# Wide attention of a two-layer decoder: the early maximum item placed behind the pass that subtracts the maxima

## The chip, the core and the metric

The kernel is one program on one NeuronCore of a Trainium2 chip. The metric is the time of one execution on the device in microseconds (us), and the figure for a kernel is the median over its runs. TensorE is called PE here, VectorE DVE, ScalarE ACT, GpSimd POOL, and PEld is TensorE's loading of weights.

## What is computed

The reference is a decoder of two layers over 1024 tokens of width 128, with a context of 6404 rows of width 96. Each layer is a self attention, a cross attention and a mixture of experts, each behind a layer norm and added to x. The change lies in the cross attention of the second layer, with 16 heads of width 64 ("wide"):

```python
q = query @ w_q                       # 1024 x 1024: 16 heads of 64
kv = context @ w_kv                   # 6404 x 2048
k, v = jnp.split(kv, 2, axis=-1)
scores = jnp.einsum('bhqd,bhkd->bhqk', q, k) * SCALE
attn = jax.nn.softmax(scores, axis=-1)
out = jnp.einsum('bhqk,bhkd->bhqd', attn, v)
return out @ w_out + b_out
```

## The kernel before

The stages run one after the other: self attention, first cross attention (small heads of 8), first experts, the second layer's attention over heads, and last `wide_heads_and_experts`, which holds the wide attention and the last experts. The wide attention takes about half of the time.

It works in 16 units. A unit is one pair of heads with one half of the tokens (512 queries), and has 51 steps, one for each block of 128 context rows, so there are 816 steps, taken in 408 pairs (`for j in range(0, STEPS, 2)`). Both heads of a pair lie in the 128 partitions, 64 for each head, and TensorE takes the two heads side by side. Query and key are each held as a high and a low part. The matmuls of one pair of steps, in program order before the change:

- `score(j)` and `score(j + 1)` (L2345): three products (high by high, low by high, high by low), each for two heads: 12 matmuls, with 64 rows of the array for each head, into PSUM banks 0 and 1 for one step and 2 and 3 for the other;
- the early item, `early[j // 2]`, when there is one: a maximum item (L2300), two matmuls of the same tiling as the scores, high part only, for a tile of 128 queries of the next unit against 512 keys. It goes to two of the three "side" banks (5 to 7), which are used in a ring;
- `subtract_maxima(j)` (L2358): four matmuls of 32 rows of the array each. They add minus the maximum to the four score banks, and their last ones release ACT by `scored`;
- `weigh(j - 2)` and `weigh(j - 1)` (L2371): probabilities times values, 128 rows by 64 columns of the array for each head, into bank 4; 8 matmul records for two steps;
- the whole items and the late items: `whole` holds now and then a fill of keys (`k`, L2318) or queries (`q`, L2311) for the next units, a turn of the maxima (`t`), a sum (`s`) or an output (`y`); `late[j // 2]` is the rest of this pair's maximum items, mostly one, in 20 places two or more.

A planner at the head of the function deals the 52 maximum items of each unit but the first out over the pairs of the unit before: 780 items, `early` takes the first of a pair (380 of them), `late` the rest (400). It also gives every item its place in the ring of three banks, in the order early, whole, late, pair after pair. A maximum item waits in `wait_place` until DVE has freed the banks, which means until the first of the two DVE reductions (L2555) of the maximum item before it, or the reading of the fill before it, is done. DVE takes, for each pair: the reductions of the early item, then an addition to the running sum (L2609) if the step is one of DVE's, the copy of the output at a unit's end (L2590), a piece of a reciprocal (L2584), then the work for the whole items (`k_lo`, L2569; `q_lo`, L2564; each behind ACT's copy of the high part, L2463 or L2460) and the reductions of the late items. ACT takes two exponentials (L2484) for each pair, then its copies for whole items. POOL adds most of the probabilities up (L2220). `score(j)` waits for the exponential of step j - 2, which used the same banks.

At the pair that follows the first step of a unit with an odd number (`between`), the late item stands between `weigh(j - 2)` and `weigh(j - 1)`, since the second has to wait until DVE has copied the last unit's output out of bank 4.

Of the kernel before, what the change touches and what calls it, by code (L numbers as in the profile page):

```python
# [1946 lines left out]
def wide_heads_and_experts(nc, name, net_name, PS, ident, ctxT, xn, xnT, x, O, A, values, out, wide):  # L1947
# [151 lines left out]
    def strip(s):  # L2099
        return slice(s * DH2, (s + 1) * DH2)  # L2100
# [4 lines left out]
    with ExitStack() as stack:  # L2105
# [160 lines left out]
        def _(pe):  # L2266
# [66 lines left out]
            def score(j):  # L2333
                n, kt = j // KT, j % KT
                p, hf, b = n // HALVES, n % HALVES, 2 * (j % 2)
                if j >= 2:
                    pe.wait_ge(exped, j - 1)
                if kt == 0:
                    pe.wait_ge(dve_freed, dve_count[("q", n)])
                if kt % 4 == 0 and hf == 0:  # L2340
                    pe.wait_ge(dve_freed, dve_count[("k", p, kt // 4)])
                keys = slice(kt * P, (kt + 1) * P)
                for k, q, start in ((k_hi, q_hi, True), (k_hi, q_lo, False), (k_lo, q_hi, False)):
                    for s in range(2):
                        pe.matmul(PS[:, b + s, :], k[p % 2][strip(s), keys], q[n % QBUFS][strip(s), :],  # L2345
                                  start=start, stop=False, tile_position=(s * DH2, 0))

            def subtract_maxima(j):

                for b in range(2):  # L2350
                    n, kt = (j + b) // KT, (j + b) % KT
                    if kt == 0:
                        pe.wait_ge(negated, negated_count[("t", n)])
                for b in range(2):
                    n, kt = (j + b) // KT, (j + b) % KT
                    for s in range(2):
                        r = 32 * (2 * b + s)
                        i = pe.matmul(PS[:, 2 * b + s, :], key_ones[r:r + 32, kt // (KT - 1), :],  # L2358
                                      minus_max[r:r + 32, n % 2, :], start=False, stop=True, tile_position=(r, 0))
                    i.then_inc(scored, 1)  # L2360

            def weigh(j):
                n, kt = j // KT, j % KT
                pe.wait_ge(exped, j + 1)
                if kt == 0 and n >= 1:
                    pe.wait_ge(out_copied, n)
                if kt % 4 == 0:
                    i = n * VF + kt // 4
                    pe.wait_ge(vals_loaded[i % VBUFS], 16 * (i // VBUFS + 1))
                for s in range(2):  # L2370
                    i = pe.matmul(PS[strip(s), PV, :], vals[:, value_slot(n, kt // 4), kt % 4, strip(s)],  # L2371
                                  prob[:, j % RING, s, :], start=(kt == 0), stop=(kt == KT - 1),
                                  tile_position=(0, s * DH2))
                i.then_inc(pv_done, 1)
# [7 lines left out]
            for j in range(0, STEPS, 2):  # L2382
                score(j)
                score(j + 1)
                for item in early[j // 2]:
                    side(item)
                subtract_maxima(j)
                between = j >= 2 and (j - 1) % KT == 0
                if j >= 2:
                    weigh(j - 2)  # L2390

                    if between:
                        assert not whole[j // 2]
                        for item in late[j // 2]:
                            side(item)
                    weigh(j - 1)
                for item in whole[j // 2] + ([] if between else late[j // 2]):
                    side(item)
                if j // KT == LAST:
                    if j % KT == NET["turn"]:  # L2400

                        pe.wait_ge(dve_freed, dve_count[("y", LAST - 1)])
                        pe.wait_ge(negated, negated_count[("s", LAST - 1)])
                        net.turn_tokens(pe, net.glue(0), 0)
                    if j % KT == NET["score"]:
                        net.score(pe, 0)
                    if j % KT == NET["turn_gates"]:
                        net.turn_gates(pe, 0)
                    if j % KT == NET["spread"]:
                        net.spread_gates(pe, 0, 0)  # L2410
# [536 lines left out]
```

## Time and profile before

| | us |
|---|---|
| median of 3 runs | 3848.77 |
| the runs | 3844.69, 3848.77, 3866.15 |
| span of the profiled execution | 3852.1 |
| mean granted TensorE clock over that span | 0.977 of full |

For the profiled execution only its span is given, from its first instruction to its last; what lies around that is not shown, and the span itself lies between the runs. In the page's slices the wide attention begins at about 1613 us with the maxima of its first unit; its steps, with maximum items beside them, go from 1667 to 3550 us, and the last unit, without maximum items, follows. A row of the timeline gives the start in us, how long the merged instructions took in us, engine, line, operation, what it writes and reads, the tile and how many; in square brackets stands idle time of the engine before it and what ended it. Matmuls are pipelined, so the durations overlap, and the distance between two starts is what a matmul takes of the engine.

### The profile page before, as it was taken

The numbers are of one execution on the slowest core, as the hardware profiler recorded it, in microseconds if no ns is written. First come the engines' busy times: TensorE is split into PE (matmuls) and PEld (weight loads), VectorE is DVE, ScalarE is ACT, GpSimd is POOL, SyncE is SP. The second block draws the span as 40 slices with busy tenths as digits, with TensorE's granted clock in tenths as the row PEclk, the third lists the DMA queues.
The fourth block names the chain that finished last, engine by engine and source line by source line (L and its number), as shares of the span: only waits on it lengthen the run. The fifth ranks groups of instructions, "written<-read, shape, count | busy, mean of one in ns | idle before, by whom it ended". The sixth has DMA issues, their size and how long they took to land.

```text
span 3852.1 us, 61024 instructions
## 1 busy us (share of the span) xinstructions
PE 3585.8 (93%) x23264; PEld 1471.9 (38%) x23264; DVE 2721.2 (71%) x4447; ACT 2164.0 (56%) x2535; POOL 2367.2 (61%) x1280
## 2 busy tenths in 40 slices
PE   6868999999999999889999999999999999999999
PEld 2332222222222244334444444444444444444444
DVE  5758888888888547776766666667666676666742
ACT  4667888888888744644444444444444444444422
POOL 3115656566565303047888888888788888889810
PEclk7969999999999999999999999999999999999999
DMA  4220001010001002500111000101010010012100
GB/s 132 52 44 8 1 10 27 1 26 11 1 1 43 10 5 87 204 14 25 29 29 29 27 28 27 30 25 32 26 29 27 28 29 28 25 55 71 30 0 6
DMA packets 74058, 126.73 MB, mean 33 GB/s; under 512 B 9875, under 2 KB 26341, under 8 KB 73093
## 3 DMA queue, kind: packets, MB, share of 16 engines
q1 hardware_dynamic: 73772, 122.82, 11.2%
q8 instruction: 191, 3.13, 0.3%
q14 instruction: 95, 0.78, 0.1%
HBM read 88.15 MB, written 34.64 MB: 32 GB/s over the span
## 4 chain that ended last, share of the span: by engine, by line
PE 51%; DVE 4%; ACT 2%; issue 1%; DVEq 0%; ACTq 0%
PE PS L2371 20%; PE PS L2345 12%; PE PS L2300 6%; PE PS L2358 5%; PE PS L2318 3%; DVE att_top_piece L2555 2%; DVE att_k_lo L2569 2%; PE PS L340 1%; PE PS L348 1%; PE PS L341 1%; ACT att_k_hi L2463 1%; PE PS L2311 0%; PE PS L2329 0%; PE PS L2323 0%; DVE att_prob L2535 0%
## 5 line engine op out<-in xcount | busy, mean ns | idle before, releaser
L2220 POOL TENSOR_TENSOR att_total<-att_total,att_prob 128x1024 f32<-128x1024 f32 x597 | 1543.7, 2586 | 352.4 <-ACT att_prob L2484 304.5
L2484 ACT ACTIVATE att_prob<-PS 128x1024 f32<-128x1024 f32 x816 | 790.9, 1021 | 1005.1 <-PE PS L2358 1005.1
L2555 DVE TENSOR_REDUCE att_top_piece<-PS 128x1 f32<-128x512 f32 (+1 forms) x1560 | 971.8, 664 | 349.6 <-PE PS L2300 339.8
L1878 DVE TENSOR_REDUCE att_top_piece<-PS 128x1 f32<-128x512 f32 (+1 forms) x1459 | 904.9, 664 | 132.4 <-PE PS L1591 127.0
L1781 ACT ACTIVATE att_prob<-PS 128x1024 f32<-128x1024 f32 (+2 forms) x912 | 892.0, 1004 | 173.5 <-PE PS L1623 170.6
L2371 PE MATMUL PS<-att_prob,att_vals 128*64 128x512 f32 x3264 | 792.0, 605 | 3.7 <-issue 2.9
L1646 PE MATMUL PS<-att_prob,cross_Vst 128*32 128x256 f32 (+1 forms) x5544 | 506.5, 431 | 2.7 <-issue 0.8
L1493 POOL TENSOR_TENSOR att_stage<-att_stage,att_run 128x512 f32<-128x512 f32 x150 | 191.4, 1276 | 401.9 <-ACT att_stage L1760 401.6
L2300 PE MATMUL PS<-att_k_hi,att_q_hi 64*128 64x512 f32 (+1 forms) x1664 | 376.3, 449 | 60.3 <-DVE att_top_piece L2555 47.0
L1591 PE MATMUL PS<-cross_Kstack,cross_Qmax 49*128 49x512 bf16 (+1 forms) x1664 | 323.5, 386 | 95.1 <-DVE att_top_piece L1878 33.4
L2345 PE MATMUL PS<-att_q_hi,att_k_hi 64*128 64x512 f32 x1632 | 329.1, 396 | 0.0
L2345 PE MATMUL PS<-att_q_hi,att_k_lo 64*128 64x512 f32 x1632 | 326.2, 391 | 0.0
L2371 PEld LDWEIGHTS PS<-att_prob,att_vals 128*64 128x64 f32 x3264 | 197.5, 136 | 335.8 <-issue 331.4
L2345 PE MATMUL PS<-att_q_lo,att_k_hi 64*128 64x512 f32 x1632 | 325.6, 391 | 0.0
L2300 PEld LDWEIGHTS PS<-att_k_hi,att_q_hi 64*128 64x128 f32 x1664 | 161.4, 185 | 416.1 <-issue 275.8
L1623 PE MATMUL PS<-cross_Qscore,cross_Kstack 49*128 49x512 bf16 x1632 | 308.6, 380 | 10.5 <-ACT att_prob L1781 6.2
L1591 PEld LDWEIGHTS PS<-cross_Kstack,cross_Qmax 49*128 49x128 bf16 x1664 | 100.3, 93 | 490.8 <-DVE att_top_piece L1878 341.3
L2609 DVE TENSOR_TENSOR k_xn<-k_xn,att_prob 128x1024 f32<-128x1024 f32 x171 | 235.2, 1375 | 13.6 <-ACT att_prob L2484 12.2
L1495 POOL TENSOR_SCALAR att_stage<-att_stage 128x512 f32<-128x512 f32 x150 | 222.6, 1484 | 13.1
L1646 PEld LDWEIGHTS PS<-att_prob,cross_Vst 128*32 128x32 f32 x5544 | 110.2, 108 | 275.2 <-ACT att_prob L1781 189.3
L2358 PE MATMUL PS<-att_minus_max,k_key_ones 32*128 32x512 f32 x1632 | 207.4, 497 | 0.0
L2569 DVE TENSOR_TENSOR att_k_lo<-PS,att_k_hi 128x512 fp32r<-128x512 f32 (+1 forms) x104 | 70.7, 680 | 192.9 <-ACT att_k_hi L2463 192.9
(316 smaller groups left out, 3394.6 us busy)
## 6 DMA issues: line engine op xcount, KB each, us to landing
att_vals<-values SPq DMA_DIRECT2D x192, 256.0 KB, 2.6
values<-att_prob SPq DMA_DIRECT2D x14, 1024.0 KB, 4.1
values<-cross_Vall SPq DMA_DIRECT2D x10, 1024.0 KB, 4.2
cross_Kstack<-kparts SPq DMA_DIRECT2D x36, 204.0 KB
f_w<-in_f_w SPq DMA_DIRECT2D x24, 256.0 KB, 3.7
kparts<-cross_Vst SPq DMA_DIRECT2D x24, 128.0 KB, 1.8
att_vals<-values SPq DMA_DIRECT2D x16, 192.0 KB, 2.3
k_ctxT<-in_ctxT SPq DMA_DIRECT2D x1, 2448.0 KB
```

The source lines that it names most:

```text
L1591: i = pe.matmul(PS[:, banks[item][s], 0:w], Qm[rows, g % 2, a, at:at + P], Kst[rows, g % 2, a, c * HALF:c * HALF + w], start=True, stop=Tr ...
L1623: i = pe.matmul(PS[:, 2 * (e % 2) + s, lo:HALF], Kst[rows, g % 2, a, kt * P:(kt + 1) * P], Qs[rows, g % 2, a, n % HALVES * HALF + lo:(n % ...
L1646: ins = pe.matmul(PS[r:r + 32, PV, lo:queries.stop], Vst[:, u % 2, kt, s, :], prob[:, j % RING, par, s, lo:queries.stop], start=(i == 0), ...
L1781: act.activation(prob[:, j % RING, par, :, lo:HALF], PS[:, 2 * (e % 2):2 * (e % 2) + 2, lo:HALF], ACT.Exp, scale=scale).then_inc(exped, 1)
L1878: dve.tensor_reduce(top_piece[:, n % 2, s * QT + qt, c:c + 1], PS[:, banks[item][s], 0:w], AX, ALU.max).then_inc(dve_freed, 1)
L2220: pool.tensor_tensor(so_far, so_far, prob[0:rows, j % RING, :, :], ALU.add).then_inc(summed, 1)
L2300: ins = pe.matmul(PS[:, bank_of(item, s), 0:w], q_hi[n % QBUFS][strip(s), qt * P:(qt + 1) * P], k_hi[p % 2][strip(s), c * HALF:c * HALF + ...
L2345: pe.matmul(PS[:, b + s, :], k[p % 2][strip(s), keys], q[n % QBUFS][strip(s), :], start=start, stop=False, tile_position=(s * DH2, 0))
L2358: i = pe.matmul(PS[:, 2 * b + s, :], key_ones[r:r + 32, kt // (KT - 1), :], minus_max[r:r + 32, n % 2, :], start=False, stop=True, tile_po ...
L2371: i = pe.matmul(PS[strip(s), PV, :], vals[:, value_slot(n, kt // 4), kt % 4, strip(s)], prob[:, j % RING, s, :], start=(kt == 0), stop=(kt ...
L2484: act.activation(prob[:, j % RING, :, :].rearrange("p a b -> p (a b)"), PSf[:, b:b + 2 * HALF], ACT.Exp, scale=scale).then_inc(exped, 1)
L2555: dve.tensor_reduce(top_piece[:, n % 2, s * QT + qt, c:c + 1], PS[:, bank_of(item, s), 0:w], AX, ALU.max).then_inc(dve_freed, 1)
```

## The change

`subtract_maxima(j)` is issued directly behind the scores, and the early item behind it instead of in front.

```diff
@@ -2382,9 +2382,9 @@
             for j in range(0, STEPS, 2):
                 score(j)
                 score(j + 1)
+                subtract_maxima(j)
                 for item in early[j // 2]:
                     side(item)
-                subtract_maxima(j)
                 between = j >= 2 and (j - 1) % KT == 0
                 if j >= 2:
                     weigh(j - 2)
```

The order of work on DVE, ACT, POOL and the DMA queue is the same in both. On PE it changes in each of the 380 pairs with an early item. The first place is a pair behind a fill of keys, in the second unit. L2345 are the scores, L2300 the maximum items, L2358 the subtraction, L2371 the weighing of the values, L2318 the fill of keys. Before:

```order
L2371 MATMUL PS<-att_prob,att_vals 64x512 x4
L2318 MATMUL PS<-k_ctxT,k_wk 128x512
L2300 MATMUL PS<-att_k_hi,att_q_hi 128x512 x2
L2345 MATMUL PS<-att_q_hi,att_k_hi 128x512 x2
L2345 MATMUL PS<-att_q_lo,att_k_hi 128x512 x2
L2345 MATMUL PS<-att_q_hi,att_k_lo 128x512 x2
L2345 MATMUL PS<-att_q_hi,att_k_hi 128x512 x2
L2345 MATMUL PS<-att_q_lo,att_k_hi 128x512 x2
L2345 MATMUL PS<-att_q_hi,att_k_lo 128x512 x2
L2300 MATMUL PS<-att_k_hi,att_q_hi 128x512 x2
L2358 MATMUL PS<-att_minus_max,k_key_ones 128x512 x4
L2371 MATMUL PS<-att_prob,att_vals 64x512 x4
```

The same pair in the changed kernel:

```order
L2371 MATMUL PS<-att_prob,att_vals 64x512 x4
L2318 MATMUL PS<-k_ctxT,k_wk 128x512
L2300 MATMUL PS<-att_k_hi,att_q_hi 128x512 x2
L2345 MATMUL PS<-att_q_hi,att_k_hi 128x512 x2
L2345 MATMUL PS<-att_q_lo,att_k_hi 128x512 x2
L2345 MATMUL PS<-att_q_hi,att_k_lo 128x512 x2
L2345 MATMUL PS<-att_q_hi,att_k_hi 128x512 x2
L2345 MATMUL PS<-att_q_lo,att_k_hi 128x512 x2
L2345 MATMUL PS<-att_q_hi,att_k_lo 128x512 x2
L2358 MATMUL PS<-att_minus_max,k_key_ones 128x512 x4
L2300 MATMUL PS<-att_k_hi,att_q_hi 128x512 x2
L2371 MATMUL PS<-att_prob,att_vals 64x512 x4
```

The maximum item that stood between scores and subtraction stands between subtraction and weighing. The second place is the one at which a maximum item stands inside the weighing, at the start of the second unit. Before:

```order
L2345 MATMUL PS<-att_q_hi,att_k_lo 128x512 x2
L2300 MATMUL PS<-att_k_hi,att_q_hi 128x512 x2
L2358 MATMUL PS<-att_minus_max,k_key_ones 128x512 x4
L2371 MATMUL PS<-att_prob,att_vals 64x512 x2
L2300 MATMUL PS<-att_k_hi,att_q_hi 128x512 x2
L2371 MATMUL PS<-att_prob,att_vals 64x512 x2
```

And in the changed kernel:

```order
L2345 MATMUL PS<-att_q_hi,att_k_lo 128x512 x2
L2358 MATMUL PS<-att_minus_max,k_key_ones 128x512 x4
L2300 MATMUL PS<-att_k_hi,att_q_hi 128x512 x2
L2371 MATMUL PS<-att_prob,att_vals 64x512 x2
L2300 MATMUL PS<-att_k_hi,att_q_hi 128x512 x2
L2371 MATMUL PS<-att_prob,att_vals 64x512 x2
```

Here too only the early item has changed its place, and the two maximum items are now nearer to each other by one subtraction.

## Rows read from the trace of the kernel before

**Rows 1.** The page's first line, and busy times of the wide stretch (stretch, PE, PEld, DVE, ACT, POOL, clock).

```profile
span 3852.1 us, 61024 instructions
...
1667.00:3550.00 1883.00, 1832.87 (x11098) 867.22 (x11095) 1290.12 (x1943) 815.42 (x893) 1541.64 (x620) 1.00 0.11 31
```

**Rows 2.** Waits of PE, 1667 to 3550: us in total, times, longest.

```profile
PE PS L2300 <- DVE att_top_piece L2555: 47.0, 116, 1.7
```

**Rows 3.** Groups by line, 1667 to 3550: the maximum items on PE, fills on DVE.

```profile
L2300 PE MATMUL PS<-att_k_hi,att_q_hi 64*128 64x512 f32 (+1 forms) x1560 | 355.8, 447 | 47.2 <-DVE att_top_piece L2555 47.0
...
L2569 DVE TENSOR_TENSOR att_k_lo<-PS,att_k_hi 128x512 fp32r<-128x512 f32 (+1 forms) x91 | 62.0, 681 | 191.8 <-ACT att_k_hi L2463 191.8
...
L2564 DVE TENSOR_TENSOR att_q_lo<-PS,att_q_hi 128x512 fp32r<-128x512 f32 x14 | 9.7, 692 | 24.7 <-ACT att_q_hi L2460 24.7
```

**Rows 4.** Timeline of PE: a pair without a wait, then one behind a fill.

```profile
2854.83 0.39 PE L2345 MATMUL PS<-att_q_hi,att_k_hi 64*128 64x512 f32 x2
...
2856.22 0.39 PE L2300 MATMUL PS<-att_k_hi,att_q_hi 64*128 64x512 f32 x2
2856.53 0.51 PE L2358 MATMUL PS<-att_minus_max,k_key_ones 32*128 32x512 f32 x4
2856.97 1.94 PE L2371 MATMUL PS<-att_prob,att_vals 128*64 128x512 f32 x8
...
2860.24 0.40 PE L2345 MATMUL PS<-att_q_hi,att_k_hi 64*128 64x512 f32 x2
...
2862.02 0.51 PE L2300 MATMUL PS<-att_k_hi,att_q_hi 64*128 64x512 f32 x2 [0.22 <-DVE att_top_piece L2555]
2862.45 0.51 PE L2358 MATMUL PS<-att_minus_max,k_key_ones 32*128 32x512 f32 x4
2862.89 1.94 PE L2371 MATMUL PS<-att_prob,att_vals 128*64 128x512 f32 x8
```

**Rows 5.** Timeline of PE: another pair behind a fill, the longer kind.

```profile
3012.64 0.40 PE L2345 MATMUL PS<-att_q_hi,att_k_hi 64*128 64x512 f32 x2
...
3014.47 0.50 PE L2300 MATMUL PS<-att_k_hi,att_q_hi 64*128 64x512 f32 x2 [0.29 <-DVE att_top_piece L2555]
...
3015.34 1.94 PE L2371 MATMUL PS<-att_prob,att_vals 128*64 128x512 f32 x8
```

**Rows 6.** Timeline of PE in the last unit, where no maximum item stands in a pair.

```profile
3554.21 0.51 PE L2345 MATMUL PS<-att_q_hi,att_k_hi 64*128 64x512 f32 x2
3554.55 0.40 PE L2345 MATMUL PS<-att_q_lo,att_k_hi 64*128 64x512 f32 x2
3554.78 0.39 PE L2345 MATMUL PS<-att_q_hi,att_k_lo 64*128 64x512 f32 x2
...
3555.79 0.51 PE L2358 MATMUL PS<-att_minus_max,k_key_ones 32*128 32x512 f32 x4
3556.23 1.94 PE L2371 MATMUL PS<-att_prob,att_vals 128*64 128x512 f32 x8
```

**Rows 7.** Timeline of PEld (weight loads), beside rows 4.

```profile
2855.99 0.19 PEld L2300 LDWEIGHTS PS<-att_k_hi,att_q_hi 64*128 64x128 f32 x2
2856.53 0.19 PEld L2358 LDWEIGHTS PS<-att_minus_max,k_key_ones 32*128 32x128 f32 x4 [0.35 <-issue]
```

**Rows 8.** Timeline of DVE, beside rows 4: behind the fill.

```profile
2860.63 0.69 DVE L2569 TENSOR_TENSOR att_k_lo<-PS,att_k_hi 128x512 fp32r<-128x512 f32 x1 [1.84 <-ACT att_k_hi L2463]
2861.24 2.61 DVE L2555 TENSOR_REDUCE att_top_piece<-PS 128x1 f32<-128x512 f32 x4
2863.77 1.21 DVE L2609 TENSOR_TENSOR k_xn<-k_xn,att_prob 128x1024 f32<-128x1024 f32 x1
```

**Rows 9.** Timeline of PE at the start of an odd unit.

```profile
2822.67 0.50 PE L2300 MATMUL PS<-att_k_hi,att_q_hi 64*128 64x512 f32 x2
2823.58 1.08 PE L2371 MATMUL PS<-att_prob,att_vals 128*64 128x512 f32 x4 [0.41 <-issue]
```

**Rows 10.** Timeline of DVE at the same place.

```profile
2821.33 1.29 DVE L2555 TENSOR_REDUCE att_top_piece<-PS 128x1 f32<-128x512 f32 x2 [0.33 <-PE PS L2300]
2822.78 0.69 DVE L2590 COPY k_O<-PS 128x512 f32<-128x512 f32 x1 [0.17 <-PE PS L2371]
```

**Rows 11.** Timeline of ACT, the exponentials of the pair in rows 4.

```profile
2857.07 1.94 ACT L2484 ACTIVATE att_prob<-PS 128x1024 f32<-128x1024 f32 x2 [2.40 <-PE PS L2358]
```

## The prediction

> **What bounds the kernel now.** I read the page first, then the busy times of the stretch in which the change acts, then PE's waits there, and last the starts on PE's timeline, pair by pair. In the 1883 us from 1667 to 3550 PE is busy for 1833, at full granted clock, beside 1290 of DVE, 815 of ACT and 1542 of POOL [rows 1]. So PE sets the time of this stretch, and every us that PE takes more or less shows in the end. All that PE waits for there is DVE's reductions, 116 times in front of a maximum item, 47.0 us together [rows 2]. ACT is not near: it sits idle for 2.40 us of each pair until the subtraction releases it [rows 11]. The change can therefore act on two things: the waits of early items, and what PE pays for a different succession of tilings. The second is not in the list of waits, since it hides in the distances between starts.
>
> **How a pair reads.** In a pair without a wait the first score matmul starts at 2854.83, the early item at 2856.22, the subtraction at 2856.53, the weighing at 2856.97 [rows 4]: 1.39 + 0.31 + 0.44 = 2.14 us. Within one tiling two matmuls side by side take 0.23 us of PE (3554.55 to 3554.78 [rows 6]). At a change of tiling two things come on top. The first step of the new kind takes 0.34 instead of 0.23 (3554.21 to 3554.55 [rows 6], scores behind a weighing): 0.11 for weights of its own that were not loaded ahead. And the last step of the old kind takes 0.31 instead of 0.23 (2856.22 to 2856.53 [rows 4]): 0.08, or rather 0.09 with the digits that rounding hides. The loads say the same: those of the early item stand at 2855.99, 0.23 us ahead of its matmul at 2856.22, while those of the subtraction start with their matmuls at 2856.53 [rows 4, 7]. A full change costs some 0.20 us. Before, a pair has three: weighing to 64 rows, 64 rows to 32 rows, 32 rows to weighing. After, it has four, since 32 rows go back to 64 rows for the early item and from there to weighing.
>
> **The price of the fourth change.** No row shows a maximum item behind a subtraction, so I put it together from neighbours. Scores straight to subtraction take 3555.79 - 3554.21 = 1.58 [rows 6], less the 0.11 of own weights, which scores behind a maximum item don't pay: 1.47. Subtraction to early item: as subtraction to weighing, 0.44 [rows 4], the nearest row, since both leave the 32 rows. Early item to weighing: as an early item whose weights weren't loaded ahead, 2862.02 to 2862.45, 0.43 [rows 4]. Sum 2.34 against 2.14: **+0.20 us**. The bounds of this price: at least nothing, if the loads and the switch hide behind running matmuls; at most 0.31, if the switch back from 32 rows costs another 0.11. I take 0.20, since each part has a row that is its like.
>
> **The waits that go.** In the pair behind a fill of keys the early item starts 1.78 us after the scores and pays for its weights as well: 2860.24 to 2862.89 is 2.65 [rows 4]; the longer kind takes 3015.34 - 3012.64 = 2.70 [rows 5]. The middle is 2.68. The cause stands on DVE: `k_lo` at 2860.63 waits for ACT's copy, the reductions of the late item follow at 2861.24, and the early item needs the first of them to be done [rows 8]. After the change the early item cannot start before 1.47 + 0.44 = 1.91 us after the scores, behind a subtraction that doesn't need DVE; the bank is free at 1.78 to 1.83 (3014.47 - 3012.64). So the wait is covered, with 0.08 us to spare, and the pair takes 2.34: **-0.34 us**. There are 91 such fills of keys and 14 of queries [rows 3], 105 pairs. (The other 11 or so of the 116 waits are those of a second late item behind a first; they stay.)
>
> **The sum.** Of the 1560 maximum matmuls, 780 items [rows 3], 380 are early. 380 - 105 = 275 pairs pay 0.20: +55.0 us. 105 pairs gain 0.34: -35.7. At the start of an odd unit, 7 times with a maximum item inside the weighing, the second weighing waits for DVE's copy of the output, which starts at 2822.78, 0.11 behind the end of the first weighing, with DVE free since 2822.62 [rows 9, 10]. The early item's reductions will then come 0.6 us later (the item starts 1.91 instead of 1.39 us after the scores, and ends 0.11 later for its weights), so DVE is free only at 2823.2 and the copy starts some 0.45 later; 0.20 of it is in the sum already, the rest is 7 x 0.25 = +1.8. The same shift on DVE is free in an ordinary pair: two reductions and an addition of 1.21 [rows 8] end some 5.0 us after the scores, the late item's reductions follow, and the next early item comes only at 4.56 + 1.91. The exponentials are released 0.31 us sooner within a pair that lasts 0.20 longer, which is worth nothing, as ACT had 2.40 us of slack [rows 11]. DMA, POOL and the order on the other queues don't change. Together 55.0 - 35.7 + 1.8 = **+21 us**. The span of 3852.1 us [rows 1] would become 3873; against the median of 3848.8, which lies 3.3 lower, it is 3870, or 0.55% more. An error of 0.01 us in the price of a pair is 4 us in the sum.
>
> **Rivals.**
> A, *the switch is free and the waits go*. Then no pair pays, the 105 gain 2.68 - 2.14 = 0.54 each: -56.7 + 1.8 = -55, **3794 us**, faster. It decides if PE can load the weights of the early item while the subtraction runs, and those of the weighing while the early item runs. For it: within one tiling the loads do run ahead by 0.23 us [rows 4, 7]. Against it: at each change of tiling that I found, they start with their own matmuls. Beside it stands a rule of the Trainium skill, "TensorE: Matmul & The Clock Gate", Part 2, step-by-step: the queue pulls weight loads ahead of running matmuls if they touch other row groups or go to the background buffer. Taken alone it gives this rival; rows 7 show it for maximum item behind scores and not for subtraction behind maximum item. "TensorEngine Tiling (Array Packing)", Key Properties, says that a change of tiling mode drains the engine, without a duration; that is the forecast's side.
>
> B, *half of the switch*: the drain of 0.09 or 0.10 is paid and the load is not. Then 275 x 0.10 - 105 x 0.44 + 1.8 = -17 us, **3832 us**, within 0.5%. It decides if one of the two (back to 64 rows, on to weighing) is cheap because both have weights across all 128 partitions. Against it: the same is so of all changes in the rows.
>
> C, *the waits stay*. The early item has only 0.08 us to spare. If DVE's chain behind a fill moves back with the pair, because ACT's copy of the high part or DVE's reductions come later than now, the 105 pairs keep their wait and pay the fourth change too: 380 x 0.20 + 1.8 = +78, **3927 us**. It decides if the first reduction of the late item ends later than 1.8 us after the scores. For it: reductions and additions on DVE stand 0.6 us later in each pair. Against it: the chain behind a fill hangs on the fill, which stands as far ahead of the next scores as before.
>
> That the change does not do what it says is excluded by the order of PE's instructions shown above.
>
> **How the numbers follow.** Forecast 0.64, A 0.10, B 0.14, C 0.12. A measurement of this kernel can tell about 0.5% from no change, here 19 us, and the forecast of 21 lies just above it; its rounding leaves 0.45 of its 0.64 above and 0.19 below. Slower: 0.45 + 0.12 = 0.57. Within 0.5%: 0.19 + 0.12 of B = 0.31. Faster: 0.10 + 0.02 of B = 0.12. The range leaves A out and most of C, and reaches to B and as far up as a quarter of the waits staying with a dearer switch (0.25 us a pair): 3834 to 3892.
>
> **What would show it.** In the changed kernel's timeline of PE: subtraction 1.47 us after the scores' start, early item 0.44 behind it, weighing 0.43 behind that; the loads of L2300 in pairs with the matmuls and not ahead of them. The waits of L2300 for L2555 fall from 116 to about 20 or fewer. A unit of 51 steps lasts some 1.4 us longer. I am wrong in the price if the early item stands much nearer than 0.44 to the subtraction or the weighing nearer than 0.43 to it (A, B), and wrong in the waits if the early item still shows idle time behind a fill (C).

## The result, and the profile after

The changed kernel takes 3982.43 us (median of 4 runs, 3972.9 to 3984.94), against 3848.07 for the kernel before in the same comparison: ratio 1.0334, 95% interval 1.0317 to 1.0352. That is slower, as forecast, but by 134 us instead of 21, and far above the range.

PE's timeline of the changed kernel, a pair without a wait; the columns are those of the timeline of before:

```profile
2928.47 0.40 PE L2345 MATMUL PS<-att_q_hi,att_k_hi 64*128 64x512 f32 x2
...
2929.97 0.50 PE L2358 MATMUL PS<-att_minus_max,k_key_ones 32*128 32x512 f32 x4
2930.40 0.50 PE L2300 MATMUL PS<-att_k_hi,att_q_hi 64*128 64x512 f32 x2
2930.83 1.94 PE L2371 MATMUL PS<-att_prob,att_vals 128*64 128x512 f32 x8
```

PEld beside it:

```profile
2929.97 0.19 PEld L2358 LDWEIGHTS PS<-att_minus_max,k_key_ones 32*128 32x128 f32 x4 [0.36 <-issue]
2930.40 0.19 PEld L2300 LDWEIGHTS PS<-att_k_hi,att_q_hi 64*128 64x128 f32 x2 [0.24 <-issue]
2930.82 0.20 PEld L2371 LDWEIGHTS PS<-att_prob,att_vals 128*64 128x64 f32 x4 [0.24 <-issue]
```

Scores to subtraction 1.50, subtraction to early item 0.43, early item to weighing 0.43: 2.36 us where the forecast had 2.34. Every load stands with its own matmul and none ahead. So the price of the fourth change of tiling came as put together.

A pair behind a fill of keys in the changed kernel, where the early item waits for nothing:

```profile
2908.37 0.39 PE L2345 MATMUL PS<-att_q_hi,att_k_hi 64*128 64x512 f32 x2
...
2909.85 0.51 PE L2358 MATMUL PS<-att_minus_max,k_key_ones 32*128 32x512 f32 x4
2910.29 0.50 PE L2300 MATMUL PS<-att_k_hi,att_q_hi 64*128 64x512 f32 x2
2910.72 1.51 PE L2371 MATMUL PS<-att_prob,att_vals 128*64 128x512 f32 x6
```

From the scores to the weighing it takes 2.35 us, where rows 4 and 5 had 2.65 and 2.70. This part of the forecast came too.

PE's waits (us in total, times, longest) did not come as forecast. The prediction had about 20 of them; rows 2 had 116, with 47.0 us. The changed kernel has:

```profile
PE PS L2300 <- DVE att_top_piece L2555: 110.9, 160, 2.6
```

The next pair of the same stretch, on PE:

```profile
2933.03 0.40 PE L2345 MATMUL PS<-att_q_hi,att_k_hi 64*128 64x512 f32 x2
...
2934.50 0.51 PE L2358 MATMUL PS<-att_minus_max,k_key_ones 32*128 32x512 f32 x4
2935.81 0.50 PE L2300 MATMUL PS<-att_k_hi,att_q_hi 64*128 64x512 f32 x2 [0.80 <-DVE att_top_piece L2555]
```

The early item stands 1.31 behind the subtraction instead of 0.43: 0.88 us are lost, and no fill stands ahead of this pair. Of the 160 waits 138 are those of an early item, and each of the 138 follows a long addition or copy on DVE in the pair before (105 without a fill ahead, 33 behind one). DVE in both pairs, and then POOL:

```profile
2930.94 1.29 DVE L2555 TENSOR_REDUCE att_top_piece<-PS 128x1 f32<-128x512 f32 x2 [0.97 <-PE PS L2300]
2932.14 2.92 DVE L2609 TENSOR_TENSOR k_xn<-k_xn,att_prob 128x1024 f32<-128x1024 f32 x1
2934.99 2.64 DVE L2555 TENSOR_REDUCE att_top_piece<-PS 128x1 f32<-128x512 f32 x4
```

```profile
2931.61 8.17 POOL L2220 TENSOR_TENSOR att_total<-att_total,att_prob 128x1024 f32<-128x1024 f32 x3 [1.26 <-ACT att_prob L2484]
```

DVE's addition, the same instruction on the same tiles, takes 2.92 us; in rows 8 it took 1.21. It starts at 2932.14, behind POOL's, which started at 2931.61. All instances over the wide attention, after (ns least/median/largest):

```profile
L2609 DVE TENSOR_TENSOR k_xn<-k_xn,att_prob x150: 1212/2918/3083, 1707.5 to 3682.1; 128x1024 f32<-128x1024 f32 x150
L2606 DVE COPY k_xn<-att_prob x15: 2362/2372/2395, 1693.7 to 3587.2; 128x1024 f32<-128x1024 f32 x15
```

and the same view of the kernel before:

```profile
L2609 DVE TENSOR_TENSOR k_xn<-k_xn,att_prob x171: 1211/1214/3429, 1701.4 to 3664.1; 128x1024 f32<-128x1024 f32 x171
L2606 DVE COPY k_xn<-att_prob x16: 681/682/693, 1687.9 to 3577.9; 128x1024 f32<-128x1024 f32 x16
```

In a pair of the kernel before, DVE comes first, by 0.33 us, and POOL is the one that is stretched: its two additions take 5.65 together, where two take 4.89 to 4.90 elsewhere. DVE's row and POOL's:

```profile
2853.51 1.22 DVE L2609 TENSOR_TENSOR k_xn<-k_xn,att_prob 128x1024 f32<-128x1024 f32 x1
```

```profile
2853.84 5.65 POOL L2220 TENSOR_TENSOR att_total<-att_total,att_prob 128x1024 f32<-128x1024 f32 x2 [1.04 <-ACT att_prob L2484]
```

The theory that this suggests: the two additions cannot run side by side, and whichever starts first holds the other off. An addition on POOL takes 2.37 to 2.39 by itself. If DVE had to wait for the end of one that started 0.53 before it, its own would take 1.84 + 1.21 = 3.05 by this estimate, and it takes 2.92. The change moves both starts, and in opposite ways. The subtraction comes 0.2 us sooner after the scores, and with it the exponential and POOL's addition; the early item's reductions, which stand ahead of DVE's addition, come 0.6 us later (over the steps up to 3500 us DVE's addition starts 3.03 us after the scores before and 3.66 after, by the median). DVE, which led by 0.33, now trails by 0.53. Its addition ends 2.9 us after its start, the late item's reductions queue behind it, and the next early item waits for the first of those. The Trainium skill has this as a rule, "SBUF — State Buffer", section "Who interferes with whom": a DVE instruction with two SBUF inputs shares a read port with a GpSimd instruction that reads SBUF, and the first to start holds it for its whole length. It says the same of DVE's copy in its two-port mode, and reductions it leaves out. The rows agree: the copy L2606 goes from 0.68 to 2.37, while the reductions L2555, which read PSUM, have a mean of 0.66 in both kernels, and the reciprocal L2584, with one input in SBUF, takes 0.94 in both, though more than half of them start while POOL adds. That the copy runs in the two-port mode no run shows. What the runs show is the collision and its order; that a port is its cause is the page's statement, and no run here separates a port from another lock.

### The profile page after: what moved, and what is told of

Its sections match the earlier page's. It is cut to its first block, busy times and chain, and to the rows that moved or that the text cites. A ratio compares the mean times of both kernels' runs of the same rounds, so it can differ in the third digit from the quotient of the medians.

```text
span 3979.7 us, 61024 instructions
## 1 busy us (share of the span) xinstructions
PE 3647.3 (92%) x23264; PEld 1470.7 (37%) x23264; DVE 2966.8 (75%) x4447; ACT 2165.0 (54%) x2535; POOL 2374.5 (60%) x1280
## 3 DMA queue, kind: packets, MB, share of 16 engines
q8 instruction: 191, 3.13, 0.3%
## 4 chain that ended last, share of the span: by engine, by line
PE 64%; DVE 22%; issue 5%; ACT 2%; DMA 0%; SPq 0%; POOL 0%; DVEq 0%; ACTq 0%; POOLq 0%
PE PS L2371 12%; DVE k_xn L2609 10%; PE PS L1646 10%; PE PS L2345 10%; PE PS L2300 7%; PE PS L1591 7%; DVE att_top_piece L2555 5%; PE PS L1623 4%; DVE att_top_piece L1878 3%; PE PS L2358 3%; PE PS L2318 2%; PE PS L546 2%; PE PS L340 1%; PE PS L559 1%; PE PS L348 1%
## 5 line engine op out<-in xcount | busy, mean ns | idle before, releaser
L2555 DVE TENSOR_REDUCE att_top_piece<-PS 128x1 f32<-128x512 f32 (+1 forms) x1560 | 970.1, 663 | 352.7 <-PE PS L2300 338.9
L2371 PE MATMUL PS<-att_prob,att_vals 128*64 128x512 f32 x3264 | 792.2, 605 | 5.0 <-ACT att_prob L2484 5.0
L2300 PE MATMUL PS<-att_k_hi,att_q_hi 64*128 64x512 f32 (+1 forms) x1664 | 404.2, 484 | 124.3 <-DVE att_top_piece L2555 110.9
L2609 DVE TENSOR_TENSOR k_xn<-k_xn,att_prob 128x1024 f32<-128x1024 f32 x171 | 468.4, 2739 | 11.4 <-ACT att_prob L2484 10.1
L2300 PEld LDWEIGHTS PS<-att_k_hi,att_q_hi 64*128 64x128 f32 x1664 | 159.3, 184 | 527.1 <-DVE att_top_piece L2555 341.0
L2345 PE MATMUL PS<-att_q_hi,att_k_hi 64*128 64x512 f32 x1632 | 329.4, 398 | 0.0
L2345 PE MATMUL PS<-att_q_hi,att_k_lo 64*128 64x512 f32 x1632 | 325.2, 392 | 0.0
L2345 PE MATMUL PS<-att_q_lo,att_k_hi 64*128 64x512 f32 x1632 | 324.6, 392 | 0.0
L2371 PEld LDWEIGHTS PS<-att_prob,att_vals 128*64 128x64 f32 x3264 | 197.6, 136 | 333.2 <-issue 286.5
L2358 PE MATMUL PS<-att_minus_max,k_key_ones 32*128 32x512 f32 x1632 | 207.7, 498 | 0.0
L1497 POOL TENSOR_TENSOR att_run<-att_run,att_stage 128x512 f32<-128x512 f32 x150 | 190.9, 1273 | 12.5
```

The costliest lines, as they stand in the source:

```text
L2300: ins = pe.matmul(PS[:, bank_of(item, s), 0:w], q_hi[n % QBUFS][strip(s), qt * P:(qt + 1) * P], k_hi[p % 2][strip(s), c * HALF:c * HALF + ...
L2555: dve.tensor_reduce(top_piece[:, n % 2, s * QT + qt, c:c + 1], PS[:, bank_of(item, s), 0:w], AX, ALU.max).then_inc(dve_freed, 1)
L2609: dve.tensor_tensor(total_dve, total_dve, now, ALU.add).then_inc(dve_summed, 1)
```

## The experiments

Each ran beside the kernel before on the same chip, and the ratios are to that one. Some chips are a little slower (the kernel before takes 3856.61 beside the first four), so ratios tell more here than times. The rival of the first four: the early item's reductions are simply too late on DVE, whatever POOL does.

**1. The changed kernel without most of POOL's additions.** From the third step of each unit POOL adds 8 of the 512 columns of each head.

```diff
-                    pool.tensor_tensor(so_far, so_far, prob[0:rows, j % RING, :, :], ALU.add).then_inc(summed, 1)
+                    few = total[0:rows, n % 2, :, 0:8]
+                    pool.tensor_tensor(few, few, prob[0:rows, j % RING, :, 0:8], ALU.add).then_inc(summed, 1)
```

> The changed kernel with POOL's additions to the running sum cut down to 8 of 512 columns from the third step of each unit on, so most of POOL's sum is left out. Theory (DVE's addition L2609 loses the SBUF port that it shares with POOL, since it now starts after POOL's addition): L2609 falls from a mean of 2.7 us back to 1.21, the waits of L2300 for L2555 fall from 160 and 111 us to some 20 waits and 25 us, and the time is that of before plus the fourth change of tiling less the waits behind fills: 3865 to 3880. Rival (the early item's reductions are simply too late on DVE, whatever POOL does): L2609 may be shorter, but the waits stay and the time stays over 3950. Rival (the fourth change of tiling costs more than the 0.20 us I took): waits go and the time stays over 3920.

Measured 3878.91 us, ratio 1.0066 (1.0042 to 1.009). DVE's addition (here L2610, as lines move by one) and PE's waits:

```profile
L2610 DVE TENSOR_TENSOR k_xn<-k_xn,att_prob x171: 1215/1216/2003, 1706.1 to 3689.2; 128x1024 f32<-128x1024 f32 x171
```

```profile
PE PS L2301 <- DVE att_top_piece L2556: 22.0, 22, 1.7
```

With POOL out of the way the addition is back at 1.21 though it starts as late as in the changed kernel (3.66 us after the scores, by the median). The waits are the 22 of a maximum item that stands right behind another, mostly of second late items, and 0.66% of 3857 is 25 us (16 to 35 by the interval), which agrees with the forecast of 21. The waits behind fills are gone, as forecast. The rival falls.

**2. Control: the kernel before with the same cut.**

> Control: the kernel before with the same cut in POOL's additions. Theory: in the kernel before DVE's addition mostly started ahead of POOL's (127 of 150 at 1.21 us), so nothing is gained: 3838 to 3852. If POOL's additions cost time by another way (ACT's ring of six probability tiles, the fold at a unit's end), this kernel becomes faster than 3835, and the first experiment's gain has to be read against it.

Measured 3855.46, ratio 0.9999 (0.9983 to 1.0015). The time in us is above the range, as this chip is slower, but the ratio is what the theory asks for: POOL's additions cost nothing before, so experiment 1 shows no general gain from an idle POOL.

**3. The changed kernel, whole, with DVE's addition ahead of the early item's reductions.**

```diff
             for j in range(0, STEPS, 2):
-                for item in early[j // 2]:
-                    side(item)
                 for i in (j - 2, j - 1):
                     if i >= 0 and dve_adds(i):
                         add(i)
+                for item in early[j // 2]:
+                    side(item)
+                for i in (j - 2, j - 1):
                     if i >= 0 and i % KT == KT - 1:
                         copy_out(i // KT)
```

> The changed kernel, whole computation, with DVE's addition put in front of the early item's reductions in DVE's order. Theory: the addition starts 1.4 to 2.3 us after the scores, when POOL is idle, and takes 1.21; the early item's reductions follow it without loss; time 3865 to 3880, with L2609 at 1.21 in nearly all of its 171 rows. Rival (reductions too late on DVE): they get later still by this order, so the time rises over 3982. Rival (the addition meets POOL at any place): L2609 stays over 2 us and the time over 3930.

Measured 3878.31, ratio 1.006 (1.0043 to 1.0078): 0.6% is 23 us over before. DVE, then POOL, at one such pair:

```profile
2871.69 1.28 DVE L2555 TENSOR_REDUCE att_top_piece<-PS 128x1 f32<-128x512 f32 x2
2872.88 1.22 DVE L2609 TENSOR_TENSOR k_xn<-k_xn,att_prob 128x1024 f32<-128x1024 f32 x1
2874.02 2.71 DVE L2555 TENSOR_REDUCE att_top_piece<-PS 128x1 f32<-128x512 f32 x4
```

```profile
2869.11 2.37 POOL L2220 TENSOR_TENSOR att_total<-att_total,att_prob 128x1024 f32<-128x1024 f32 x1 [0.55 <-ACT att_prob L2484]
2873.80 5.07 POOL L2220 TENSOR_TENSOR att_total<-att_total,att_prob 128x1024 f32<-128x1024 f32 x2 [2.32 <-ACT att_prob L2484]
```

The addition starts in the gap between POOL's last addition of the pair before and its first of this one. It leads that one by 0.92 us and keeps its 1.22, and POOL's two take 5.07. PE's order is that of the changed kernel, the early item's reductions are if anything later, and some 105 us are back. PE waits as in experiment 1:

```profile
PE PS L2300 <- DVE att_top_piece L2555: 21.9, 22, 1.7
```

I was wrong in one thing: not nearly all additions are at 1.21. The ones that start 1.4 us after the scores can still meet the end of POOL's addition; the median is 1.22, but 70 of the 148 up to 3560 us started while POOL was busy and took 1.60 on average. No early item waits for them.

**4. Control: the kernel before with the same order on DVE.**

> Control: the kernel before with the same order on DVE. Theory: additions were not in POOL's way before, so nothing moves: 3840 to 3856. If the order on DVE were worth something by itself (earlier or later release of side banks), this one would show it.

Measured 3861.83, ratio 1.0018 (0.9999 to 1.0037), and 6 us above the range. There is no gain, and perhaps a loss of a few us (the waits for L2555 are 125 with 49.8 us), so the order by itself doesn't explain what experiment 3 gave back.

**5. The loss without the change.** PE's order is that of before; only DVE's addition is held back until POOL's has started. The tile `idle` and its semaphore are new; the two small memsets stand only for delay.

```diff
                     if i >= 0 and dve_adds(i):
+                        dve.wait_ge(exped, j + 1)
+                        for again in range(2):
+                            dve.memset(idle[:, :], 0.0).then_inc(idled, 1)
+                            idles[0] += 1
+                            dve.wait_ge(idled, idles[0])
                         add(i)
```

> The kernel before, PE's order untouched, whole computation; DVE's addition waits in addition for the first exponential of its own pair and for two small memsets (64 columns), so that it starts after POOL's addition, which the same exponential releases. Theory (port): L2609 goes to 2.5 to 3.2 us in most rows, the late item's reductions and the next early item behind it are held up by up to 2 us in about 130 pairs, time 3980 to 4120. Rival (what hurts is only how PE's early item and subtraction stand): no more than the 0.5 us by which the addition is late, which DVE's slack covers: 3845 to 3870.

Measured 4184.42, ratio 1.0869 (1.085 to 1.0888). DVE and POOL, and PE's waits:

```profile
2909.95 0.30 DVE L2619 MEMSET att_idle<- 128x64 f32 x2 [0.25 <-ACT att_prob L2485]
2910.29 3.13 DVE L2610 TENSOR_TENSOR k_xn<-k_xn,att_prob 128x1024 f32<-128x1024 f32 x1
```

```profile
2909.95 2.39 POOL L2221 TENSOR_TENSOR att_total<-att_total,att_prob 128x1024 f32<-128x1024 f32 x1 [3.60 <-ACT att_prob L2485]
```

```profile
PE PS L2301 <- DVE att_top_piece L2556: 247.9, 219, 3.0
```

An addition that starts 0.34 us behind POOL's takes 3.13 instead of 1.21, and the kernel before loses 8.7% with no matmul moved. My upper end (4120) was too low. The waits for L2555 grow by 201 of the 329 us that the span grows by. Much of the rest goes with the granted clock, which falls from 0.977 to 0.959 of full: that is some 166 us more at the lower of its two levels (1.2 instead of 2.4 GHz), which by my estimate costs up to 83 us. That the waits are longer than in the changed kernel, since the early item has no subtraction in front of it that covers the delay, is argued and not tested.

**6. Control for 5, with POOL's additions cut as in 1.**

> Control: the same, with POOL's additions cut down to 8 columns from the third step of each unit on (most of POOL's sum left out). Theory: the addition is as late but takes 1.21, so the lateness alone costs little: 3845 to 3875. If lateness alone were the cost, this would be as slow as the kernel with whole additions on POOL.

Measured 3865.57, ratio 1.0039 (1.0025 to 1.0053). The addition is as late (3.69 us after the scores in both, by the median) and costs 0.39%; the other 8.3% of experiment 5 come from the collision, the lower clock that follows it included.

**7. The exchange only behind fills.** This was the part of the change that promised something.

```diff
+                behind_fill = j >= 2 and any(item[0] in ("q", "k") for item in whole[j // 2 - 1])
+                if behind_fill:
+                    subtract_maxima(j)
                 for item in early[j // 2]:
                     side(item)
-                subtract_maxima(j)
+                if not behind_fill:
+                    subtract_maxima(j)
```

> The exchange of subtraction and early item only in the 105 pairs that follow a fill of keys or queries; elsewhere the order of before; DVE as before. Theory: 105 pairs gain 0.33 us (-35), but in about a third of them DVE has an addition, which now meets POOL's and holds up the next pair by up to 1.5 us: 3855 to 3885. If the port plays no part here: 3812 to 3825.

Measured 3872.59, ratio 1.0049 (1.0032 to 1.0067). Waits of PE:

```profile
PE PS L2300 <- DVE att_top_piece L2559: 62.3, 62, 2.6
```

The waits behind fills are gone, but where DVE has an addition in such a pair it meets POOL's, and the next pair pays. There are 41 waits of early items, and each follows a pair behind a fill with a long addition. Pairs not behind a fill lose 46 us together, pairs behind one gain 31.

**8. The same with DVE's addition in front, as in 3.**

> The same selective exchange, and DVE's addition in front of the early item's reductions. Theory: the waits behind fills go (-35), no pair pays a fourth change of tiling without gaining, the addition keeps clear of POOL's long hold: 3812 to 3832, faster than both kernels. Against the changed kernel with the same order on DVE (3878) the difference is the 275 x 0.20 = 55 us of the fourth change in pairs without a wait, which measures that price. If the price were smaller, the difference is smaller.

Measured 3825.95, ratio 0.993 (0.9915 to 0.9944): faster than both kernels. Against experiment 3, which differs only in the pairs that are not behind a fill, it is 1.3% of 3852, or 50 us, over 275 pairs: 0.18 us each for the fourth change of tiling, where I had 0.20. The two intervals leave about 0.15 to 0.21; the traces are sharper. From scores to weighing these pairs take 2.14 us in this kernel and 2.35 in that of experiment 3, by the median.

**9 and 10. DVE's addition in front only behind fills, beside a repeat of 8 on one chip.**

> The exchange behind fills only, and DVE's addition in front of the early item's reductions in those pairs only; elsewhere both orders of before. Theory: in other pairs the addition starts 3.03 us after the scores, just ahead of POOL's, at 1.21; behind fills it starts at about 2.0 and takes 1.21 to 2. So L2609 is at 1.21 in nearly all rows, and the time is that of the version with the addition in front everywhere, or up to 5 us less: 3815 to 3832.

> The same kernel as the selective exchange with the addition in front everywhere, beside the other version on one chip: ratio to before 0.990 to 0.995 again.

Measured 3821.98, ratio 0.9908 (0.9889 to 0.9927), and 3826.72, ratio 0.9931 (0.9913 to 0.9948). The version with both selections is the best of these; its lead over 8 is inside the intervals. In it DVE's addition and PE's waits read:

```profile
L2613 DVE TENSOR_TENSOR k_xn<-k_xn,att_prob x171: 1212/1216/3431, 1709.5 to 3643.3; 128x1024 f32<-128x1024 f32 x171
```

```profile
PE PS L2300 <- DVE att_top_piece L2559: 23.4, 27, 1.7
```

The median addition is at 1.22 and the waits behind fills are gone, as experiment 9 had to show. The largest, 3.43 us, is as in the kernel before.

## Why the prediction was wrong

**What bounds the kernel: right.** PE sets the time, and the loss showed as PE's waits and distances. One reading was too round: PE waits there not only for DVE's reductions but also 7 times, 2.9 us together, for the second weighing at the start of an odd unit.

**The price of the fourth change: right.** 2.36 us in the trace for the forecast 2.34, 2.35 by the median of these pairs in experiments 1 and 3, and 0.18 a pair by the times of experiments 3 and 8. Both rivals on its side fell: the switch is neither free (A) nor half price (B).

**The waits behind fills: right** where nothing else meets them. Experiments 1 and 3 have 22 waits instead of 116, and come out at +25 and +23 us, where the sum said +21. The split of the 116 was off: the trace has 95 behind fills and 21 elsewhere, not 105 and 11. The other 10 pairs behind a fill show no wait in the list and take 2.42; over all 105 the mean is 2.68, as the sum had it. The third term, +1.8, is too small for the times to tell; PE's waits in front of L2371 go from 3.7 to 5.0 us.

**The step that failed** is the sentence "The same shift on DVE is free in an ordinary pair: two reductions and an addition of 1.21 [rows 8] end some 5.0 us after the scores". I moved the addition by 0.6 us and kept its duration, read from a place where it led POOL's (2863.77 in rows 8, against 2864.10 on POOL). The sentences beside it failed with it: the sooner exponentials were not "worth nothing", since POOL's addition starts on them, and "POOL ... don't change" holds for its order, not for its times. With 2.9 instead of 1.21 the same working gives what the pair shows: the addition ends 3.7 + 2.9 = 6.6 us after the scores, the first reduction of the late item 0.7 later, which is 2.7 us into the next pair of 4.56, and the early item that could start there at 1.91 starts at 2.78 (2935.81 less 2933.03). The profile of before carried the warning in two places: 5.65 us for two additions on POOL beside rows 8's kind of addition on DVE, and a largest L2609 of 3429 ns over a least of 1211 (that one in the last unit; up to 3550 us the largest is 1952).

**The account of the gap.** Between experiment 1 and the changed kernel lie 102.5 us of span (3877.2 and 3979.7). PE's waits for L2555 differ by 110.9 - 22.0 = 88.9 us. The list understates each wait by about 0.08 (0.80 in brackets, 0.88 by the starts), which over 138 more waits is 11. The 3 us that are left are within what runs of one kernel differ by (3870 to 3889 in experiment 1).

**How much of the loss the forecast had.** Its mechanism, a dearer succession of tilings less the waits behind fills, makes some 25 of the 134 us, as experiments 1 and 3 show. So the direction, slower, would have come by it alone; the rest is the collision, which it did not have.

**Rival C** had the symptom, early items waiting on DVE, and 78 us; its cause was wrong. The waits came back behind stretched additions, mostly where no fill stands ahead, and experiments 1 and 3 show the chain behind a fill in time.

## What to carry to other kernels

Before moving an instruction in one engine's queue, list what runs on DVE and POOL at the same time, and which of the two starts first: here DVE's addition, with both inputs in SBUF, kept its 1.21 us only where it led POOL's or POOL was idle. A reordering on PE alone can turn that order round, as here, where it moved what releases POOL and what releases DVE in opposite directions. Where a move gains in some pairs only, do it in those pairs only: here the selective version turned +3.3% into -0.9%.

## What I had not expected of the hardware

A lead of 0.33 us or a lag of 0.53 us between two additions decides between 1.21 and 2.92 us for the one on DVE, while POOL's loses less than a microsecond when it comes 0.33 us behind (5.65 for two instead of 4.9). A change of the array's tiling costs 0.18 to 0.20 us here, of which 0.09 is time between matmuls and 0.11 a weight load that isn't hidden, and neither shows as idle time in the list of waits. With 64 columns of weights, as in the weighing, the load costs 0.05 (0.48 from its first step to the second, then 0.43).
